# The second group norm's statistics in an attention and conditional-convolution kernel: one ScalarE square around the channel mean instead of VectorE's batch-norm instructions

## Chip, cores and metric

The kernel runs on one NeuronCore of a Trainium2 chip. The metric is the device time of one execution in microseconds; shown are the median and the ends of three runs. The profile is one further execution. In it PE is TensorE, DVE is VectorE, ACT is ScalarE, POOL is GpSimd and SP is SyncE, the engine that issues the transfers.

## What is computed

Sixteen images x of 128 channels and 32x32 pixels pass through two residual blocks. Each block begins with a group norm over 32 groups of four channels. The core of the reference:

```python
x = x + _L0_conv_ref(_gn(x), g1, w_qkv, mem_kv, w_out, b_out, g2)
x = x + _L1_conv_ref(_gn(x), expert_weight, rconv_w, rconv_b, fc_w, fc_b)

def _gn(v, G=32, eps=1e-05):
    g = v.reshape(B_, G, C_ // G, H_, W_)
    m = jnp.mean(g, axis=(2, 3, 4), keepdims=True)
    s = jnp.var(g, axis=(2, 3, 4), keepdims=True)
    return ((g - m) / jnp.sqrt(s + eps)).reshape(v.shape)
```

`_L0_conv_ref` is linear attention with four heads: an RMS norm over channels, projections to q, k and v, a softmax of q over channels and of k over pixels, a context matrix, an output projection and a second RMS norm. `_L1_conv_ref` pools the normed image to 4x4 cells, computes from them three gates per output channel (the routing), mixes three 3x3 filters by these gates, and convolves the image with the mix.

The change concerns the second `_gn`: mean and variance of each channel of the image `x2`, the sum of x and the attention's output. Averages over the four channels of a group are then taken by a small matmul.

## The kernel before

The kernel is a software pipeline over the 16 images, with an order written out by hand for each engine in a function `step(t, p)`. In step t different stages work on different images: the projections and the first norm's application on image t-1, the attention's context and output on image t-2, the second norm, the routing and the filters' mix on image t-3, the convolution on image t-4. An engine takes its instructions strictly in the written order. Between engines there are only semaphores: `do(part, t, p, age)` emits a part for image t-age, and a part begins with its waits. Steps 9 to 14 are a loop of three rounds of two steps; the others are written out. Tiles lie as 128 channels (partitions) by 1024 pixels, or as eight tiles of 128 pixels by 128 channels.

The stretch of a step that the change touches, engine by engine:

- VectorE forms `x2` (`residual1`, L902). Then `gn2_stats` (L904 to L910) takes batch-norm statistics of its two halves, `rms1` (L782) averages eight columns of square sums of another image (GpSimd's `rms1` waits for them, and ScalarE's `qkv_evacuate` for that), and `gn2_aggregate` (L912 to L917) writes mean and variance of each channel to `meanvar[:, 1, :]`. `gn2_pool` (L919) sums `x2` over 4x4 cells for the routing. Then come `means` (L750), which waits for the group means, `k_sums`, `differences`, `gn2_centre`, `spreads` (L766), `context_mask`, `variances` and `mix_evacuate`.
- TensorE's `group_means` (L1099 to L1112) averages the means of four channels each. It waits for `meanvar2_done` and stands between the two halves of `q_transpose` (L1181), behind `key_context_transpose` (L1163). Behind these come `contexts` (L1165 to L1169), which waits for `x_k_done`, then `project` for tile 1, `group_variances`, `mixes`, more projections and `outputs` (L1191). The 54 matmuls of the convolution are strewn between all of these, and the conv matmuls are in the same strict order.
- ScalarE evacuates the key contexts (`k_x_evacuate`, L613), copies the second half of the transposed image (`x_copy`, L575), evacuates the transposed contexts (`x_k_evacuate`, L619, for which `contexts` waits), then the transposed q (L625) and the projected tiles (L594).

Of the kernel before, what the change touches and what calls it, by code (L numbers as in the profile page):

```python
# [25 lines left out]
def attention_condconv_kernel(  # L26
# [38 lines left out]
    with ctx:  # L65
# [6 lines left out]
        def sem(name):  # L72
            return ctx.enter_context(nc.semaphore(name))
# [77 lines left out]
        stats2 = sb("stats2", [128, 2, 6])  # L151
# [69 lines left out]
        stats2_read = sem("stats2_read")  # L221
# [45 lines left out]
        stats2_done = sem("stats2_done")  # L267
# [288 lines left out]
        def _(act):  # L556
# [3 lines left out]
            def squares1(b, p, h):  # L560

                act.wait_ge(x_t_ps, 2 * b + h + 1)
                if past(b, 1):
                    act.wait_ge(ssq1_done, b)
                    act.wait_ge(ssq1_sum_done, 2 * b)
                for t in range(NT // 2 * h, NT // 2 * (h + 1)):
                    last = nc.scalar.activation(squares[:, tile(t)], ps_qkv[h][:, tile(t % (NT // 2))], ACT.Square,  # L567
                                                accum_out=ssq1_sum[:, t:t + 1])
                last.then_inc(ssq1_sum_done, 1)
# [67 lines left out]

            def image_high(b, p):
# [39 lines left out]
            def step(t, p):  # L678
# [18 lines left out]
                do(k_x_evacuate, t, p, 2)  # L697
                do(x_copy, t, p, 1, 1)
# [16 lines left out]
        def _(dve):  # L715
# [188 lines left out]
            def gn2_stats(b, p):  # L904
                dve.wait_ge(x2_done, b + 1)
                if past(b, 1):
                    dve.wait_ge(meanvar2_done, b)
                for h in range(2):
                    last = v.bn_stats(stats2[:, h, :], x2[p][:, half(h)])
                last.then_inc(stats2_done, 1)  # L910

            def gn2_aggregate(b, p):  # L912
                if past(b, 1):
                    dve.wait_ge(gmean_ps, b + GAP)
                    dve.wait_ge(spread_done, b + GAP)
                dve.wait_ge(stats2_done, b + 1).then_inc(stats2_read, 1)
                v.bn_aggr(meanvar[:, 1, :], stats2[:, :, :].rearrange("p h s -> p (h s)")).then_inc(meanvar2_done, 1)  # L917

            def gn2_pool(b, p):  # L919
                dve.wait_ge(x2_done, b + 1)  # L920
                if past(b, 1):
                    dve.wait_ge(pooled_c_done, b)
                v.tensor_reduce(pooled[:, :].rearrange("p (i j) -> p i j", j=SP),
                                x2[p][:, :].rearrange("p (i a j b) -> p i j a b", i=SP, j=SP, b=W // SP), AX.XY, ALU.add).then_inc(pooled_done, 1)

# [97 lines left out]
            def step(t, p):  # L1023
# [8 lines left out]
                do(gn2_stats, t, p, 3)  # L1032
                do(rms1, t, p, 1)
                do(gn2_aggregate, t, p, 3)
                do(gn2_pool, t, p, 3)
# [282 lines left out]
```

## Time and profile before

| what | us |
|---|---|
| median of three runs | 458.72 (458.58 to 461.26) |
| the profiled execution's own time | 460.76 |
| its span, first to last instruction | 459.0 |
| TensorE busy | 413.5 |
| VectorE busy | 356.3 |
| ScalarE busy | 294.7 |
| GpSimd busy | 262.2 |

The profiled execution has 1.76 us outside its span. "Busy" counts the time in which at least one instruction of the engine runs. A timeline row gives start, length, engine, line and operation, with the output left of the arrow; square brackets give idle time ahead of it and what ended that. Lines are those of the kernel before.

### The profile page before, as it was taken

Reading aid. Unit: us, or ns where it says so; the run is one execution under the profiler, and the core shown is the slowest. Engines: PE = TensorE matmul, PEld = TensorE weight load, DVE = VectorE, ACT = ScalarE, POOL = GpSimd, SP = SyncE. Lnnn points to the kernel's source line nnn. Section 1 sums busy time; section 2 is a strip of 40 time slices with the busy share of each in tenths; the row PEclk is TensorE's granted clock in tenths of the full one; section 3 lists DMA queues with packets and bytes.
Section 4 is the critical chain, followed back from the end, with each engine's and each line's share of the span. In section 5 each row is a group of like instructions: output and inputs, shape, how many; then the busy total and the mean of one; then the engine's idle time right before and its main releaser. Section 6 shows DMA issues by size and latency. Waiting matters only on the chain.

```text
span 459.0 us, 8623 instructions
## 1 busy us (share of the span) xinstructions
PE 413.5 (90%) x2478; PEld 358.3 (78%) x2478; DVE 356.3 (78%) x773; ACT 294.7 (64%) x903; POOL 262.2 (57%) x249
## 2 busy tenths in 40 slices
PE   2476686789999999999999999999999999999896
PEld 1466585678989898988888798989898989787675
DVE  3265578979798979888897979898989796977710
ACT  2336566676867686868686787868686868644221
POOL 4326354855758493949494757667684847334130
PEclk9997858699999999999999999999999999999899
DMA  6302024222625243343425061626262423342331
GB/s 194 162 0 94 1 93 183 91 94 91 230 93 217 106 174 149 142 181 128 194 91 230 34 244 43 237 83 228 91 229 91 171 106 131 145 157 120 142 133 46
DMA packets 18786, 61.61 MB, mean 134 GB/s; under 512 B 2992, under 2 KB 4032, under 8 KB 18752
## 3 DMA queue, kind: packets, MB, share of 16 engines
q1 hardware_dynamic: 18752, 61.21, 35.5%
q8 instruction: 15, 0.25, 0.2%
q14 instruction: 19, 0.16, 0.1%
HBM read 19.29 MB, written 8.39 MB: 60 GB/s over the span
## 4 chain that ended last, share of the span: by engine, by line
PE 60%; DVE 13%; issue 10%; ACT 8%; DMA 4%; POOL 1%; SPq 1%; DVEq 0%; ACTq 0%; POOLq 0%
PE ps_conv L1227 26%; PE ps_att L1158 6%; PE ps_y L1191 6%; PE ps_y L1197 3%; PE ps_qkv L1137 3%; PE ps_y L1181 3%; DVE w_full L1008 2%; DMA xa<-in_x_dram 2%; PE ps_qkv L1139 2%; PE ps_qkv L1138 2%; ACT expert_raw L655 2%; DMA expert_raw<-_conv_expert_weight_dram 2%; ACT squares L567 2%; PE ps_qkv L1124 2%; DVE route_terms L956 2%
## 5 line engine op out<-in xcount | busy, mean ns | idle before, releaser
L594 ACT ACTIVATE qk<-ps_qkv,scale 128x256 f32<-128x256 f32 x128 | 56.4, 470 | 10.8 <-PE ps_qkv L1139 8.8
L537 POOL TENSOR_TENSOR left_hi<-zeros 128x32 fp32r<-128x32 f32 x16 | 5.7, 358 | 80.0 <-DMA right_lo<-img_lo 80.0
L661 ACT ACTIVATE w_hi<-w_full 128x1152 fp32r<-128x1152 f32 x16 | 18.7, 1167 | 50.7 <-DVE w_full L1014 50.7
L530 POOL TENSOR_TENSOR w_lo<-w_full,w_hi 128x1152 fp32r<-128x1152 f32 x16 | 42.8, 2677 | 12.7 <-ACT w_hi L661 7.7
L485 POOL TENSOR_TENSOR x_lo<-x,x_hi 128x1024 fp32r<-128x1024 f32 x16 | 38.3, 2393 | 16.1 <-ACT x_hi L584 16.1
L1137 PE MATMUL ps_qkv<-wqk_hi,x_hi 128*128 128x256 f32 x128 | 42.3, 331 | 5.7 <-ACT qk L594 3.7
L511 POOL TENSOR_TENSOR scale<-ssq,minus_half 128x8 f32<-128x8 f32 x16 | 26.2, 1638 | 34.4 <-DVE ssq L883 34.4
L635 ACT ACTIVATE y_scaled<-ps_y 128x128 f32<-128x128 f32 x128 | 33.3, 292 | 14.7 <-PE ps_y L1191 14.7
L1227 PE MATMUL ps_conv<-right_lo,w_hi 128*128 128x512 f32 (+1 forms) x96 | 41.7, 435 | 0.0
L1227 PE MATMUL ps_conv<-img_hi,w_hi 128*128 128x512 f32 x96 | 39.3, 410 | 2.1 <-POOL w_lo L530 1.8
L1227 PE MATMUL ps_conv<-right_hi,w_lo 128*128 128x512 f32 (+1 forms) x96 | 38.7, 403 | 0.0
L1227 PE MATMUL ps_conv<-right_hi,w_hi 128*128 128x512 f32 (+1 forms) x96 | 37.8, 394 | 0.0
L1227 PE MATMUL ps_conv<-left_lo,w_hi 128*128 128x512 f32 (+1 forms) x96 | 37.7, 393 | 0.0
L1227 PE MATMUL ps_conv<-img_hi,w_lo 128*128 128x512 f32 x96 | 37.7, 392 | 0.0
L1227 PE MATMUL ps_conv<-img_lo,w_hi 128*128 128x512 f32 x96 | 37.6, 392 | 0.0
L1227 PE MATMUL ps_conv<-left_hi,w_lo 128*128 128x512 f32 (+1 forms) x96 | 37.5, 390 | 0.0
L1139 PE MATMUL ps_qkv<-wqk_hi,x_lo 128*128 128x256 f32 x128 | 37.3, 292 | 0.0
L1227 PE MATMUL ps_conv<-left_hi,w_hi 128*128 128x512 f32 (+1 forms) x96 | 37.3, 388 | 0.0
L1138 PE MATMUL ps_qkv<-wqk_lo,x_hi 128*128 128x256 f32 x128 | 37.2, 290 | 0.0
L670 ACT ACTIVATE expert_raw<-ps_conv,gmean 128x512 f32<-128x512 f32 x32 | 21.7, 678 | 23.9 <-PE ps_conv L1227 23.8
L567 ACT ACTIVATE squares<-ps_qkv 128x128 f32<-128x128 f32 x128 | 32.4, 259 | 6.8 <-PE ps_qkv L1124 6.8
L1158 PE MATMUL ps_att<-x_nt,k_exp 128*128 128x130 f32 x256 | 34.7, 293 | 0.0
(149 smaller groups left out, 1322.8 us busy)
## 6 DMA issues: line engine op xcount, KB each, us to landing
xa<-in_x_dram SPq DMA_DIRECT2D x16, 512.0 KB, 4.3
xb<-in_x_dram SPq DMA_DIRECT2D x16, 512.0 KB, 4.8
out_dram<-expert_raw SPq DMA_DIRECT2D x16, 512.0 KB, 2.9
left_hi<-img_hi SPq DMA_DIRECT2D x16, 511.5 KB, 3.1
right_hi<-img_hi SPq DMA_DIRECT2D x16, 511.5 KB, 4.0
left_lo<-img_lo SPq DMA_DIRECT2D x16, 511.5 KB, 2.9
right_lo<-img_lo SPq DMA_DIRECT2D x16, 511.5 KB, 3.7
expert_raw<-_conv_expert_weight_dram SPq DMA_DIRECT2D x1, 1728.0 KB, 9.3
```

What stands on the lines that cost most here:

```text
L485: nc.gpsimd.tensor_tensor(x1_lo[:, :], x1[:, :], x1_hi[:, :].bitcast(F32), ALU.subtract).then_inc(x1_lo_done, 1)
L511: nc.gpsimd.tensor_tensor(scale2[:, :], ssq2[:, :], minus_half[:, :], ALU.pow).then_inc(scale2_done, 1)
L530: nc.gpsimd.tensor_tensor(w_lo[p][:, :, :].rearrange("p t o -> p (t o)"), w_full[:, :], w_hi[p][:, :, :].bitcast(F32).rearrange("p t o -> ...
L567: last = nc.scalar.activation(squares[:, tile(t)], ps_qkv[h][:, tile(t % (NT // 2))], ACT.Square, accum_out=ssq1_sum[:, t:t + 1])
L594: nc.scalar.activation(qk[:, t, :], ps_qkv[t % 2][:, 0:QK], ACT.Copy, scale=scale1[:, t:t + 1]).then_inc(qkv_done, 1)
L635: last = nc.scalar.activation(y_scaled[:, t, :], ps_y[:, tile(t)], ACT.Square, accum_out=ssq2_sum[:, t:t + 1])
L1137: mm(o, x1_hi[:, tile(t)], wqk_hi[:, :], start=True, stop=False)
L1138: mm(o, x1_hi[:, tile(t)], wqk_lo[:, :], start=False, stop=False)
L1139: mm(o, x1_lo[:, tile(t)], wqk_hi[:, :], start=False, stop=True).then_inc(qkv_ps, 1)
L1158: last = mm(ps_att[:, 0:CEXT], k_exp[:, t, :], x_nt[p][:, t, :], start=False, stop=(t == NT - 1))
L1191: last = mm(ps_y[:, tile(t)], q_t[p][:, tile(t)], mix[p][:, :], start=True, stop=True)
L1227: last = mm(into, weight[:, tap, :], pixels[:, top + down:bottom + down, :], start=(n == 0), stop=(n == 3 * TAPS - 1))
```

## The change

Mean and variance of a channel no longer come from VectorE's batch-norm instructions. `gn2_pool` moves up to stand directly behind `residual1`. A new `gn2_sum` adds the 16 cell sums of a channel to one number, and a new `gn2_average` writes two multiples of it: the channel's mean to `meanvar[:, 1, 0:1]`, and minus the mean over the square root of N = 1024 to `centre_bias`. A new part on ScalarE, `gn2_variance`, reads all of `x2` once, squares it with scale 1/32 and this bias, and lets the accumulator sum the squares: that sum is the channel's variance. The full-size output goes to `squares`, a scratch tile that the first RMS norm also uses. The part stands between `k_x_evacuate` and the second `x_copy`. `meanvar2_done`, for which TensorE's `group_means` waits, is now raised by it. TensorE's, GpSimd's and SyncE's orders stay as they were.

```diff
@@ ScalarE
             def squares1(b, p, h):
                 act.wait_ge(x_t_ps, 2 * b + h + 1)
+                if past(b, 3):
+                    act.wait_ge(meanvar2_done, b - 2)
...
+            def gn2_variance(b, p):
+
+                act.wait_ge(centre_bias_done, b + 1)
+                act.wait_ge(ssq1_sum_done, 2 * (b + 3) if not isinstance(b, int) else 2 * min(b + 3, B))
+                if past(b, 1):
+                    act.wait_ge(spread_done, b + GAP)
+                nc.scalar.activation(squares[:, :], x2[p][:, :], ACT.Square, bias=centre_bias[:, :], scale=1.0 / N ** 0.5,
+                                     accum_out=meanvar[:, 1, 1:2]).then_inc(meanvar2_done, 1)
...
                 do(k_x_evacuate, t, p, 2)
+                do(gn2_variance, t, p, 3)
                 do(x_copy, t, p, 1, 1)
@@ VectorE
-            def gn2_stats(b, p):
-                dve.wait_ge(x2_done, b + 1)
-                if past(b, 1):
-                    dve.wait_ge(meanvar2_done, b)
-                for h in range(2):
-                    last = v.bn_stats(stats2[:, h, :], x2[p][:, half(h)])
-                last.then_inc(stats2_done, 1)
-
-            def gn2_aggregate(b, p):
-                if past(b, 1):
-                    dve.wait_ge(gmean_ps, b + GAP)
-                    dve.wait_ge(spread_done, b + GAP)
-                dve.wait_ge(stats2_done, b + 1).then_inc(stats2_read, 1)
-                v.bn_aggr(meanvar[:, 1, :], stats2[:, :, :].rearrange("p h s -> p (h s)")).then_inc(meanvar2_done, 1)
-
...
+            def gn2_sum(b, p):
+                dve.wait_ge(pooled_done, b + 1)
+                if past(b, 1):
+                    dve.wait_ge(centre_bias_done, b)
+                v.tensor_reduce(pooled_sum[:, :], pooled[:, :], AX.X, ALU.add).then_inc(pooled_sum_done, 1)
+
+            def gn2_average(b, p):
+
+                dve.wait_ge(pooled_sum_done, b + 1)
+                if past(b, 1):
+                    dve.wait_ge(meanvar2_done, b)
+                    dve.wait_ge(gmean_ps, b + GAP)
+                    dve.wait_ge(dev_done, b + GAP)
+                v.tensor_scalar(meanvar[:, 1, 0:1], pooled_sum[:, :], 1.0 / N, None, ALU.mult)
+                v.tensor_scalar(centre_bias[:, :], pooled_sum[:, :], -1.0 / (N * N ** 0.5), None, ALU.mult).then_inc(centre_bias_done, 1)
...
                 do(residual1, t, p, 3)
-                do(gn2_stats, t, p, 3)
+                do(gn2_pool, t, p, 3)
+                do(gn2_sum, t, p, 3)
+                do(gn2_average, t, p, 3)
                 do(rms1, t, p, 1)
-                do(gn2_aggregate, t, p, 3)
-                do(gn2_pool, t, p, 3)
                 turn(means, t, p, 0)
```

VectorE's row in the program before, in the loop, from the forming of `x2` to the group means (`ssq` is `rms1`'s output, `x_1` is one of the two `x2` buffers):

```order
L902 SCALAR_TENSOR_TENSOR x_1<-ps_y,g_c,xb 128x1024
L909 BN_STATS stats<-x_1 128x6 x2
L787 TENSOR_SCALAR ssq<-ssq_sum 128x8
L917 BN_AGGR meanvar<-stats 128x2
L923 TENSOR_REDUCE pooled<-x_1 128x16
L759 TENSOR_SCALAR nmean<-ps_stat 128x2
```

and in the changed program, where line numbers after the first edits are some lines higher:

```order
L915 SCALAR_TENSOR_TENSOR x_1<-ps_y,g_c,xb 128x1024
L921 TENSOR_REDUCE pooled<-x_1 128x16
L928 TENSOR_REDUCE pooled_sum<-pooled 128x1
L937 TENSOR_SCALAR meanvar<-pooled_sum 128x1
L938 TENSOR_SCALAR centre_bias<-pooled_sum 128x1
L800 TENSOR_SCALAR ssq<-ssq_sum 128x8
L772 TENSOR_SCALAR nmean<-ps_stat 128x2
```

The pooling has moved ahead of `rms1`; two reads of the whole tile by BN_STATS and the BN_AGGR are gone, and three small instructions on one or 16 columns stand in their place. ScalarE's row before, from the results' evacuation in the same step:

```order
L670 ACTIVATE expert_raw<-ps_conv,gmean_1 128x512
L613 ACTIVATE k_x<-ps_att 128x130
L575 ACTIVATE x_nt<-ps_qkv 128x4x128
L619 ACTIVATE x_k<-ps_att 128x128
L625 ACTIVATE q_t<-ps_y 128x512
L594 ACTIVATE qk<-ps_qkv,scale 128x256 x2
L625 ACTIVATE q_t<-ps_y 128x512
```

and in the changed program:

```order
L682 ACTIVATE expert_raw<-ps_conv,gmean_1 128x512
L616 ACTIVATE k_x<-ps_att 128x130
L647 ACTIVATE squares,meanvar<-x_1,centre_bias 128x1024
L578 ACTIVATE x_nt<-ps_qkv 128x4x128
L622 ACTIVATE x_k<-ps_att 128x128
L628 ACTIVATE q_t<-ps_y 128x512
L597 ACTIVATE qk<-ps_qkv,scale 128x256 x2
L628 ACTIVATE q_t<-ps_y 128x512
```

The square on 1024 columns now stands ahead of the second copy to `x_nt`, the evacuation of `x_k` and the evacuation of q.

## Rows read from the trace of the kernel before

**Rows 1.** The page: busy us, share of the span and instructions by engine.

```profile
PE 413.5 (90%) x2478; PEld 358.3 (78%) x2478; DVE 356.3 (78%) x773; ACT 294.7 (64%) x903; POOL 262.2 (57%) x249
```

**Rows 2.** Stretches: length; busy and count of PE, PEld, DVE, ACT, POOL; clock; DMA share, GB/s.

```profile
145.63:169.53 23.90, 23.90 (x154) 21.02 (x154) 20.87 (x47) 17.94 (x57) 15.61 (x15) 1.00 0.39 143
...
241.90:266.71 24.81, 24.16 (x154) 21.00 (x154) 21.32 (x47) 17.86 (x57) 15.58 (x15) 1.00 0.38 143
...
290.79:315.26 24.47, 24.19 (x154) 21.00 (x154) 21.87 (x48) 18.23 (x57) 15.83 (x15) 1.00 0.40 149
```

**Rows 3.** Timeline of VectorE, 162 to 167 us: start, length, engine, line, operation.

```profile
162.76 1.22 DVE L902 SCALAR_TENSOR_TENSOR x<-ps_y,g_c,xb 128x1024 f32<-128x1024 f32 x1
164.02 1.29 DVE L909 BATCH_NORM_STATS2 stats<-x 128x6 f32<-128x512 f32 x2
165.22 0.15 DVE L787 TENSOR_SCALAR ssq<-ssq_sum 128x8 f32<-128x8 f32 x1
165.49 0.21 DVE L917 BATCH_NORM_AGGREGATE meanvar<-stats 128x2 f32<-128x12 f32 x1
165.62 1.20 DVE L923 TENSOR_REDUCE pooled<-x 128x16 f32<-128x1024 f32 x1
166.73 0.15 DVE L759 TENSOR_SCALAR nmean<-ps_stat 128x2 f32<-128x2 f32 x1
```

**Rows 4.** Timeline of TensorE, the same step.

```profile
166.33 0.28 PE L1112 MATMUL ps_stat<-meanvar,group_avg 128*128 128x2 f32 x2
166.47 0.63 PE L1181 MATMUL ps_y<-ident,q_exp 128*128 128x128 f32 x4
166.94 0.41 PE L1168 MATMUL ps_att<-memk_exp,memv_t 128*128 128x128 f32 x2
```

**Rows 5.** Timeline of ScalarE, the same step, and two rows from 160 us.

```profile
160.57 0.25 ACT L567 ACTIVATE squares<-ps_qkv 128x128 f32<-128x128 f32 x1
160.73 0.19 ACT L567 ACTIVATION_READ_ACCUMULATOR squares<-ps_qkv 128x1 f32 x1
...
165.20 0.28 ACT L613 ACTIVATE k_x<-ps_att 128x130 f32<-128x130 f32 x1 [0.34 <-PE ps_att L1158]
165.37 0.60 ACT L575 ACTIVATE x_nt<-ps_qkv 128x512 f32<-128x512 f32 x1
166.53 0.28 ACT L619 ACTIVATE x_k<-ps_att 128x128 f32<-128x128 f32 x1 [0.56 <-PE ps_att L1163]
```

**Rows 6.** Groups by line, the nearest relatives: line, operands, count, busy us, mean ns.

```profile
L813 DVE TENSOR_REDUCE k_max<-ps_att 128x1 f32<-128x128 f32 x16 | 4.5, 281 | 0.0
...
L1021 DVE TENSOR_SCALAR gmean<-nmean 128x1 f32<-128x1 f32 x16 | 2.3, 145 | 0.0
...
L731 DVE TENSOR_REDUCE memk_max<-mem_c 128x1 f32<-128x4 f32 x1 | 0.1, 136 | 0.0
```

**Rows 7.** Groups by line on ScalarE, the nearest relative of the square.

```profile
L642 ACT ACTIVATE img_hi<-x,nmean 128x1024 fp32r<-128x1024 f32 x16 | 18.4, 1149 | 3.3 <-DVE nmean L759 3.3
```

**Rows 8.** Timeline of the step around 91 us, ScalarE and TensorE.

```profile
90.87 0.28 ACT L613 ACTIVATE k_x<-ps_att 128x130 f32<-128x130 f32 x1 [1.74 <-PE ps_att L1158]
...
92.61 0.41 PE L1168 MATMUL ps_att<-memk_exp,memv_t 128*128 128x128 f32 x2
```

**Rows 9.** Timeline of the last two steps of the second norm.

```profile
404.57 1.22 DVE L902 SCALAR_TENSOR_TENSOR x<-ps_y,g_c,xb 128x1024 f32<-128x1024 f32 x1
...
408.28 0.39 PE L1168 MATMUL ps_att<-memk_exp,memv_t 128*128 128x128 f32 x2
...
426.40 0.21 DVE L917 BATCH_NORM_AGGREGATE meanvar<-stats 128x2 f32<-128x12 f32 x1 [0.19 <-DVE stats L909]
...
426.67 0.38 PE L1112 MATMUL ps_stat<-meanvar,group_avg 128*128 128x1 f32 x2
...
427.64 0.15 DVE L759 TENSOR_SCALAR nmean<-ps_stat 128x1 f32<-128x1 f32 x1
```

**Rows 10.** Timeline of VectorE, the latest arrival of an input image.

```profile
243.49 1.28 DVE L740 BATCH_NORM_STATS2 stats<-xa 128x6 f32<-128x512 f32 x2 [2.08 <-DMA xa<-in_x_dram]
```

More of the change, by code:

```diff
@@ L150, in attention_condconv_kernel @@
         x2 = [sb(f"x2_{p}", [128, N]) for p in range(2)]
-        stats2 = sb("stats2", [128, 2, 6])
+        pooled_sum = sb("pooled_sum", [128, 1])
+        centre_bias = sb("centre_bias", [128, 1])
         pooled = sb("pooled", [128, SP * SP])
@@ L220, in attention_condconv_kernel @@
         ssq1_sum_done = sem("ssq1_sum_done")
-        stats2_read = sem("stats2_read")
         x1_done = sem("x1_done")
@@ L266, in attention_condconv_kernel @@
         x2_done = sem("x2_done")
-        stats2_done = sem("stats2_done")
+        pooled_sum_done = sem("pooled_sum_done")
+        centre_bias_done = sem("centre_bias_done")
         meanvar2_done = sem("meanvar2_done")
```

## Prediction

> **What bounds the kernel now.** I read the page's busy shares first. TensorE is busy for 413.5 us of a span of 459.0, 90%; VectorE for 356.3 us (78%), ScalarE for 294.7 (64%) [rows 1]. Then I cut the middle of the run into stretches from one start of `outputs` (L1191) to the next, which is one step of the pipeline. The stretch from 145.63 to 169.53 is 23.90 us long and TensorE is busy for all 23.90 of it, at a granted clock of 1.00 (2.4 GHz). In this step TensorE waits for nobody, and any time that it is made to wait is added to the step. The stretches from 241.90 and from 290.79 are longer, 24.81 and 24.47 us, with 0.65 and 0.28 us in which TensorE has no work [rows 2]. That is the only kind of slack the middle has. So the question is not how much work VectorE loses and ScalarE gains, but when TensorE's next instruction may start.
>
> Last I read the timelines of one full step, engine by engine, around the place of the change. `x2` starts at 162.76, takes 1.22 and is ready at 163.98. The batch-norm statistics start at 164.02 and the aggregate ends at 165.49 + 0.21 = 165.70 [rows 3]. `group_means` runs at 166.33 [rows 4]: it has 0.63 us in hand. Behind it the second half of the q transposes starts at 166.47 and `contexts` at 166.94. ScalarE in the same stretch evacuates `k_x` from 165.20 to 165.48, copies to `x_nt` from 165.37 to 165.97, then waits 0.56 us for the transpose and evacuates `x_k` from 166.53 to 166.81 [rows 5]. `contexts` starts 0.13 us after that. So two chains meet TensorE here, and each has little in hand: statistics to `group_means`, and `k_x` to `x_k` to `contexts`.
>
> **The change, part by part.** *Removed on VectorE:* the statistics (1.29 for the pair) and the aggregate (0.21). *Moved:* the pooling, 1.20 us, which stood behind the aggregate, now stands ahead of everything that `group_means` needs. *Added on VectorE:* one sum over 16 columns and two TENSOR_SCALARs on one column. The trace has no 16-column sum; its bounds are 0.14 us (four columns) and 0.28 (128 columns) [rows 6]. I take 0.16, near the first. A one-column TENSOR_SCALAR takes 0.145 [rows 6]; the second can overlap with the first, so the pair takes between 0.2 and 0.3 and I take 0.23. *Added on ScalarE:* a square on 1024 columns with a bias column. Its nearest relative is `image_high`, with the same input, size and kind of bias, 1.149 us [rows 7]. An accumulating square is followed by a read of the accumulator; on 128 columns that starts 0.09 us ahead of the square's end (160.73 against 160.57 + 0.25) and takes 0.19 [rows 5]. So the pair ends 1.25 us after its start, and the next instruction can start after 1.15.
>
> *The new chain in this step.* `x2` ends at 163.98; the pooling runs from 164.02 to 165.22; the sum ends at 165.42 (0.04 us between dependent instructions, as between `x2`'s end and the statistics' start [rows 3]); the two multiples end at 165.69. ScalarE has been free since 165.48 and starts the square at 165.72. The accumulator is out at 166.97. TensorE follows the last aggregate of the run by 0.06 us (426.40 + 0.21 against 426.67 [rows 9]), so `group_means` starts at 167.03 in place of 166.33: 0.70 later.
>
> *What queues behind the square on ScalarE.* The second `x_nt` copy starts at 166.87 in place of 165.37. It takes 0.60, of which 0.1 is overlapped, so `x_k` starts at about 167.35 and ends at 167.63. `contexts` starts at 167.68 by this path, and by the other at 167.03 + 0.61 (its distance from `group_means` before, 166.94 against 166.33 [rows 4]) = 167.64. Both say 0.74 later. What follows on ScalarE (q's evacuation, the projected tiles) moves by no more than that, and TensorE asks for it 0.74 later too. `rms1` on VectorE slips from 165.22 [rows 3] to about 165.75; GpSimd's reciprocal square root and the scaled evacuation behind it slip by 0.5, less than TensorE. The group means are read by VectorE at about 167.35 instead of 166.73 [rows 3], a slip of 0.6. I cost all of these at nothing, because TensorE's own 0.74 hides them; if that cover were gone, each would cost its own slip. The new waits in `squares1` are for something done most of a step earlier.
>
> *The saved VectorE time.* Per step 1.50 us go and 0.39 come, 1.1 saved. It falls into the time in which VectorE waits for the group means, so I count it at nothing.
>
> Here a page speaks against the small instructions. The row for one column is 0.145 us [rows 6]. The Trainium skill, "VectorE: DVE Perf Modes", section on the TRN2 errata, says that an instruction reading SBUF pays a fixed cost, put at 58 cycles of 0.96 GHz beside its columns, and advises tiles of at least 512 elements so that the cost is spread. An estimate by that page gives 0.08 us for the sum and 0.06 for each multiple, and the step's loss would be some 0.2 us smaller; the page's figure is less than half of the row, the measurement decides, and its advice points the same way as the row.
>
> **The sum.** The second norm runs in 16 steps.
> - Eight are like the one above: 8 x 0.74 = 5.9.
> - In five others `k_x` ends later against `x2`, and ScalarE would have started the square later than VectorE lets it, but all else was later too. In the one at 91 us `k_x` ends at 91.15, the square runs to 92.40, the copy starts at 92.30, `x_k` ends at 93.08, and `contexts` starts at 93.14 in place of 92.61 [rows 8]: 0.53. I take this for all five: 2.7.
> - In the first step of the second norm TensorE is later still: 0.1 by the same working, an estimate from the last case.
> - In the last but one there is no `x_nt` copy and no `rms1`, and TensorE stood at `contexts` at 408.28, 3.71 after the start of `x2` at 404.57 [rows 9]. The new chain puts it at 167.68 - 162.76 = 4.92 after: 1.2.
> - In the last there is no `k_x`. `group_means` slips to `x2` plus 4.3, 427.9 in place of 426.67, but VectorE read it only at 427.64 because the pooling was in the way [rows 9]. Now it reads it at about 428.3: 0.7 on a chain that ends the kernel.
>
> Together 10.6 us. Back come at most the idle 0.65 and 0.28 of rows 2: there an image landed late (VectorE waited 2.08 us for it [rows 10]), and its load is issued ahead of the new delay, so a later TensorE finds it there. I take 0.8. The net is +9.8 us: 460.76 for the profiled execution becomes 470.6, and the median of 458.72, 2.04 below the profiled one, becomes 468.5.
>
> *Bounds of the unknown.* With the lower ends (0.14, 0.2, and a square of 1.05) a step loses about 0.15 less, -2.2 us in all. With the upper ones (0.28, 0.3, 1.25) it loses 0.3 more, +4.5. The forecast's own range is therefore 465.5 to 473.
>
> **Rivals.** A measurement of this kernel can tell about 1% from no change, so the bounds are 463 and 454 us.
> - *Hidden.* The modelled ends of the matmuls make TensorE look fuller than it is, and there is half a microsecond of slack somewhere in each step. Then a step loses 0.1 to 0.2 and the kernel 2 to 4 us with the last steps: 461.5. For it: the ends of the matmuls are modelled, so 23.90 of 23.90 may hold small gaps. Against it: the `k_x` to `contexts` chain gives 0.13 us of room only [rows 4, 5]. 10%.
> - *VectorE pays back: faster.* If VectorE paces the step, from the routing's sums through the filters and the softmax to `x2`, each step gets the 1.1 us that it saves, less the 0.74 lost if ScalarE's square still reaches TensorE, and 16 x 0.4 = 6 us less gives 452. It decides from the point at which VectorE has no idle time around `group_means`. Against it: the work saved stands behind that chain, not in it, and VectorE is busy for only 20.87 of 23.90 [rows 2]. 3%.
> - *The delay spreads.* The square also pushes the scale of the projected tiles and the q evacuation past the point where TensorE needs them, or holds back the shifted images. A second loss of 0.4 us per step gives 16 x 0.4 = 6.4 more: 475. Against it: the slips worked out above are all under 0.74. 11%.
> - *The clock falls.* All stretches of rows 2 have 1.00, the one with 0.65 us of idle TensorE too, so a stall of 0.74 should change nothing. If it did and each of 16 steps ran 2 us at 1.2 GHz, 1 us more per step would give 484. The Trainium skill, "TensorE: Matmul & The Clock Gate", Part 1, says that the array's clock is halved after idle time; this trace shows no such fall at stalls of this size. 1%.
>
> That the change does not do what it says is no likely rival: mean and variance come out of the same numbers, with the same instruction count for TensorE.
>
> **How the numbers follow.** The forecast has 75%: 468.5. The range reaches down into the hidden case and up into the spreading one, 463.0 to 475.0. Slower by over 1%: the forecast, the spreading, the clock, 87%, less a few for a forecast that ends under 463: 0.85. Within 1%: the hidden case and those few, 0.12. Faster: 0.03.
>
> **What would show it.** In the changed profile TensorE should wait at `group_means` or `contexts` in about 15 steps, 0.6 to 0.8 us each, for ScalarE's square or for `x_k`; the square should take 1.15 us and start 0.2 us or so behind the end of `k_x`; the step that was 23.90 us should be 24.6. VectorE should wait for the group means by about 1.4 us, where it waited for nothing. If that step is still under 24.1, the hidden case is right. If TensorE's new waits stand at projections or at the convolution, the delay has spread. If VectorE's end of `x2` comes earlier against TensorE, the saved time was worth something.

## The result and the profile after

The changed kernel takes 469.19 us (median of four runs, 468.44 to 469.82), the kernel before, run beside it, 459.99. The ratio is 1.0195, with a 95% interval of 1.0141 to 1.0248: slower by 9.2 us. The forecast was 468.5, 9.8 above the 458.72 from which it started. The profiled execution took 469.82 us with a span of 468.1; the forecast for it was 470.6. Ratios and intervals leave out runs more than 1.5% above the fastest run of the same kernel; of all kernels here only one, the pooling first with the average early, has such runs.

The page's busy row, which answers to [rows 1]:

```profile
PE 417.4 (89%) x2478; PEld 360.1 (77%) x2478; DVE 339.9 (73%) x773; ACT 311.9 (67%) x935; POOL 266.2 (57%) x249
```

VectorE has 16.4 us less to do and ScalarE 17.2 more, and the span is 9.1 longer. TensorE has the same 2478 matmuls; its busy time is 3.9 us more. The mean granted clock is 0.956 in place of 0.963, and the first matmuls behind a wait show as longer ones (the pair of the group means 0.35 us in place of 0.28); how the 3.9 us divide between the two was not worked out.

Stretches between two starts of `outputs` (now L1205), as in [rows 2] (length; busy and count of PE, PEld, DVE, ACT, POOL; clock; DMA):

```profile
144.92:169.56 24.64, 24.18 (x154) 21.06 (x153) 20.56 (x48) 19.11 (x59) 16.84 (x15) 1.00 0.40 153
...
244.31:269.73 25.42, 24.17 (x155) 21.07 (x153) 20.98 (x48) 19.10 (x59) 16.55 (x15) 1.00 0.38 144
...
294.69:320.06 25.37, 24.26 (x155) 21.03 (x154) 20.95 (x48) 19.14 (x59) 15.85 (x15) 1.00 0.38 143
```

The step that was 23.90 us with TensorE full is 24.64 with 24.18 busy. The two long ones are 25.42 and 25.37 in place of 24.81 and 24.47. They have 0.46, 0.60 and 0.83 us more without work on TensorE than the same steps before; the rest of the loss, at most 0.28 us, shows as longer busy time. The granted clock is 1.00 in all of them.

VectorE's timeline of one step, which answers to [rows 3]:

```profile
162.15 1.22 DVE L915 SCALAR_TENSOR_TENSOR x<-ps_y,g_c,xb 128x1024 f32<-128x1024 f32 x1
163.41 1.22 DVE L921 TENSOR_REDUCE pooled<-x 128x16 f32<-128x1024 f32 x1
164.67 0.17 DVE L928 TENSOR_REDUCE pooled_sum<-pooled 128x1 f32<-128x16 f32 x1
164.87 0.15 DVE L937 TENSOR_SCALAR meanvar<-pooled_sum 128x1 f32<-128x1 f32 x1
164.94 0.14 DVE L938 TENSOR_SCALAR centre_bias<-pooled_sum 128x1 f32<-128x1 f32 x1
165.00 0.22 DVE L800 TENSOR_SCALAR ssq<-ssq_sum 128x8 f32<-128x8 f32 x1
166.85 0.16 DVE L772 TENSOR_SCALAR nmean<-ps_stat 128x2 f32<-128x2 f32 x1 [1.63 <-PE ps_stat L1126]
```

The pooling is behind `x2` at once; the sum (L928) starts 2.52 us after the start of `x2`, the second multiple ends at 2.93. `nmean` now waits 1.63 us for the group means, where [rows 3] had no wait. That is where VectorE's saved time went: in this step it stands idle there. ScalarE in the same step, as in [rows 5]:

```profile
164.69 0.28 ACT L616 ACTIVATE k_x<-ps_att 128x130 f32<-128x130 f32 x1 [0.45 <-PE ps_att L1172]
165.12 1.15 ACT L647 ACTIVATE squares<-x,centre_bias 128x1024 f32<-128x1024 f32 x1
166.18 0.19 ACT L647 ACTIVATION_READ_ACCUMULATOR squares<-x,centre_bias 128x1 f32 x1
166.27 0.58 ACT L578 ACTIVATE x_nt<-ps_qkv 128x512 f32<-128x512 f32 x1
166.75 0.27 ACT L622 ACTIVATE x_k<-ps_att 128x128 f32<-128x128 f32 x1
```

The square starts 0.04 us after `centre_bias`, runs 1.15, and the accumulator is out at 166.37, 4.22 after the start of `x2`. The copy to `x_nt` stands behind it, and `x_k` starts 4.60 after the start of `x2`, where it was 3.77. TensorE, as in [rows 4]:

```profile
166.46 0.35 PE L1126 MATMUL ps_stat<-meanvar,group_avg 128*128 128x2 f32 x2 [0.44 <-issue]
166.68 0.64 PE L1195 MATMUL ps_y<-ident,q_exp 128*128 128x128 f32 x4
167.15 0.40 PE L1182 MATMUL ps_att<-memk_exp,memv_t 128*128 128x128 f32 x2
```

Against the start of `x2` the group means are at 4.31 in place of 3.57 and `contexts` (L1182) at 5.00 in place of 4.18. The view of waits on TensorE says how often:

```profile
PE ps_stat L1126 <- issue: 7.1, 13, 0.9
...
PE ps_stat L1126 <- ACT squares L647: 2.5, 3, 1.2
```

Together 9.6 us in all 16 steps, from 0.16 to 1.24 us each. The "issue" of the first row is not idle sequencing: in the step above the row carries "issue" and yet the matmul starts 0.09 us after the accumulator's read. I read it as a wait whose releaser the profile could not name. The prediction had asked for waits of 0.6 to 0.8 us in about 15 steps. VectorE's side of the same thing (it was 9.0 us in 5 waits before):

```profile
DVE nmean L772 <- PE ps_stat L1126: 35.9, 19, 3.4
```

### The profile page after: what moved, and what is told of

Read it like the earlier page. It is cut to its first block, busy times and chain, and to the rows that moved or that the text cites. A ratio compares the mean times of both kernels' runs of the same rounds, so it can differ in the third digit from the quotient of the medians.

```text
span 468.1 us, 8702 instructions
## 1 busy us (share of the span) xinstructions
PE 417.4 (89%) x2478; PEld 360.1 (77%) x2478; DVE 339.9 (73%) x773; ACT 311.9 (67%) x935; POOL 266.2 (57%) x249
## 4 chain that ended last, share of the span: by engine, by line
PE 66%; DVE 13%; issue 11%; ACT 5%; DMA 2%; SPq 1%; POOL 1%; DVEq 0%; ACTq 0%
PE ps_conv L1241 29%; PE ps_y L1205 6%; PE ps_att L1172 6%; PE ps_y L1195 3%; PE ps_y L1211 3%; PE ps_qkv L1151 3%; PE ps_qkv L1153 2%; PE ps_qkv L1152 2%; DVE w_full L1022 2%; ACT expert_raw L667 2%; DMA expert_raw<-_conv_expert_weight_dram 2%; PE ps_stat L1218 2%; ACT qk L597 2%; PE ps_qkv L1138 1%; PE ps_stat L1126 1%
## 5 line engine op out<-in xcount | busy, mean ns | idle before, releaser
L538 POOL TENSOR_TENSOR left_hi<-zeros 128x32 fp32r<-128x32 f32 x16 | 7.1, 447 | 80.5 <-DMA right_lo<-img_lo 80.5
L1241 PE MATMUL ps_conv<-left_hi,w_lo 128*128 128x512 f32 (+1 forms) x96 | 37.9, 394 | 0.0
```

The source lines that it names most:

```text
L1241: last = mm(into, weight[:, tap, :], pixels[:, top + down:bottom + down, :], start=(n == 0), stop=(n == 3 * TAPS - 1))
```

## The experiments

All runs are compared with the kernel before on the same chip. `x2`+4.3 means 4.3 us after the start of `x2` in that step. "Over the twelve steps" means from the start of the third `x2` to that of the last but one, in the profiled execution: 290.28 us before and 298.96 in the changed kernel, 8.7 more. Behind some medians this length is given, because the stretch ahead of the third `x2` varies from kernel to kernel by more than the steps do (see the end).

**Pooling first.** Is the lateness of the statistics alone enough?

```diff
                 do(residual1, t, p, 3)
+                do(gn2_pool, t, p, 3)
                 do(gn2_stats, t, p, 3)
-                do(rms1, t, p, 1)
                 do(gn2_aggregate, t, p, 3)
-                do(gn2_pool, t, p, 3)
+                do(rms1, t, p, 1)
```

> The kernel before with one edit in VectorE's order: the pooling stands ahead of the batch-norm statistics, and the averaging of the square sums behind the aggregate, as in the change. ScalarE has no new work. Theory (the loss is lateness of the channel statistics and of x_k at TensorE): the aggregate ends 1.1 us later, about 4.1 us after the start of x2, so the group means start 4.15 after it in place of 3.57, TensorE waits 0.6 us there in most of the 16 steps, and the time is 8 us above the kernel before. Rival (the loss is ScalarE's square in its queue alone, the group means had room): no change within 2 us, and no wait at the group means.

Measured: 469.5 us, ratio 1.0215 (1.0148 to 1.0282). So a mere change of order on VectorE, with no new work anywhere, costs as much as the whole change (10.6 us over the twelve steps). Its waits on TensorE:

```profile
PE ps_stat L1112 <- issue: 4.0, 10, 0.6
...
PE ps_stat L1112 <- DVE meanvar L917: 2.4, 3, 1.1
```

That is 6.4 us at the group means, in 13 steps; they start at `x2`+4.16, as worked out. The rival is out. But `outputs` was 0.7 to 0.85 us late, not 0.6, and the time 2 us over what was expected.

**The same with the average of the square sums early.** One line differs: `do(rms1, t, p, 1)` stands between `gn2_stats` and `gn2_aggregate` again.

> The pooling-first run cost 10 us, not 8: TensorE started the group means 0.6 us late but the outputs 0.8 to 0.85 late. Its averaging of the square sums stood behind the aggregate, 1.7 us later than before. Here it stands ahead of the aggregate, as in the kernel before, and the pooling still stands first. Theory (the extra 0.15 to 0.2 us per step came from that averaging, through GpSimd's reciprocal root to ScalarE's scaled evacuations): group means at about 4.2 us after the start of x2, outputs 0.65 later than before and not 0.85, the time 1.5 to 3 us under the pooling-first run. Rival (the extra comes from the late group means themselves, by way of the spreads): the outputs stay 0.85 late and the time is the same within 1 us.

Measured: median of all ten runs 466.29 us, ratio 1.0109 (1.0061 to 1.0156). The group means are still at `x2`+4.16, `outputs` at 7.24 in place of 7.45 to 7.60. So the extra did come with the late average; that it goes by way of GpSimd and the scaled evacuations was expected and not looked at by itself. The ten runs fall into two groups, five from 461.6 to 464.3 and five from 468.2 to 469.4, and the profile, 468.92, is of the upper one. So the size of the gain is not told by the median. The steps tell it: over the twelve steps this kernel loses 5.7 us, 4.9 less than the run before.

**A square beside.** Is what queues behind the square on ScalarE enough? The statistics stay on VectorE; the sum of this square is read by nobody.

```diff
+            def square_beside(b, p):
+
+                act.wait_ge(x2_done, b + 1)
+                act.wait_ge(ssq1_sum_done, 2 * (b + 3) if not isinstance(b, int) else 2 * min(b + 3, B))
+                if past(b, 1):
+                    act.wait_ge(beside_done, b)
+                nc.scalar.activation(squares[:, :], x2[p][:, :], ACT.Square, bias=g2_c[:, :], scale=1.0 / N ** 0.5,
+                                     accum_out=unused_sum[:, :]).then_inc(beside_done, 1)
...
                 do(k_x_evacuate, t, p, 2)
+                do(square_beside, t, p, 3)
```

> The kernel before with the statistics as they were, and beside them a full-size ScalarE square with accumulator at the changed kernel's place, behind the evacuation of k_x, whose sum nobody reads. Only what queues behind it on ScalarE is late. Theory: the square starts when the k_x evacuation ends, 2.7 us after the start of x2, the evacuation of x_k starts 4.35 after it in place of 3.77, and the contexts 4.7 in place of 4.18: 0.5 us in each of 15 steps, so 7 us above the kernel before, with TensorE's wait at the contexts and none at the group means. Rival (only the wait for the statistics costs): no change within 2 us. If this and the pooling-first run each give 7 to 8, the two paths run side by side in the change and do not add up, since the change costs 9 to 10.

Measured: 464.58 us, ratio 1.0122 (1.006 to 1.0185), 5 us and not 7. In the usual step the square starts at `x2`+2.61, `x_k` at 4.22 and `contexts` at 4.55, 0.36 late. I had started the square at the end of the `k_x` evacuation; ScalarE overlaps two instructions by 0.1 us, at both ends of the square. TensorE's wait stands where it should, at `contexts`, short but in 14 steps:

```profile
PE ps_att L1182 <- ACT x_k L623: 2.8, 14, 0.3
```

**Half the square.** Does the loss follow the square's length? (The variance is that of half the image's sum; the rest is as in the change.)

```diff
-                nc.scalar.activation(squares[:, :], x2[p][:, :], ACT.Square, ...
+                nc.scalar.activation(squares[:, 0:N // 2], x2[p][:, 0:N // 2], ACT.Square, ...
```

> The changed kernel with the square over only the first 512 of 1024 pixels of each channel; the variance is then that of half the image's sum. Theory (a step's loss follows the square's length): the square is 0.43 to 0.5 us shorter, group means and contexts come earlier by as much, each of 16 steps loses 0.3 in place of 0.75, and the time is 7 us under the changed kernel, about 462 where before is 460. Rival (what costs is the longer VectorE chain and the extra semaphore hand-over, not the square's length): under 2 us less than the changed kernel.

Measured: 460.99 us, ratio to before 1.0037 (1.0002 to 1.0072), 8 us under the changed kernel, where 7 were expected. The square takes 0.72 in place of 1.15 us, and group means and `contexts` come at `x2`+3.88 and 4.57, each 0.42 us earlier. Over the twelve steps the kernel loses 3.6 us in place of 8.7: 0.43 us less per step, which is the time by which the square is shorter. The other 3 us or so lie outside these steps: in its profile the third `x2` starts at 108.28, in that of the changed kernel at 112.71.

**Wait for the mean only.** The group means read `meanvar[:, c, 0]`, the mean; the variance is first read by `spreads`.

```diff
-                    pe.wait_ge(meanvar2_done, j + 1 - GAP)
+                    pe.wait_ge(centre_bias_done, j + 1 - GAP)
...
             def spreads(j, p):
...
+                if past(j, GAP):
+                    dve.wait_ge(meanvar2_done, j + 1 - GAP)
```

> The changed kernel with the wait put where the number is needed: TensorE's group means read only the mean, so they wait for VectorE's average, and VectorE's spreads, which read the variance, wait for the square. The square stays at its place on ScalarE. Theory (two paths side by side): the group means start at 3.57 after the start of x2 as before and TensorE does not wait there, but the evacuation of x_k still starts at 4.6, so the contexts start at 4.9 to 5.0 as in the changed kernel: the wait moves from the group means to the contexts and the time stays within 2 us of the changed kernel's 469. Rival (the wait at the group means is the whole cost): 7 to 9 us less, the time of before.

Measured: 467.45 us, ratio 1.019 (1.0128 to 1.0253). The group means are at `x2`+3.57 again, TensorE waits there for nobody, and `contexts` is at 4.91. The wait has moved one place on, nearly whole:

```profile
PE ps_att L1184 <- ACT x_k L622: 8.3, 15, 0.9
```

With the pooling-first run this is the core of the matter. Over the twelve steps the late `x_k` alone costs 7.9 us (here; 3.1 with the square beside, which starts earlier), the late statistics alone 5.7 (with the average early), and both together 8.7: they run side by side and do not add up. In time, 467.45 is 1.7 us under the changed kernel, which the intervals of the two do not tell from nothing.

**The square one place further back.** Built on the mean-wait kernel: `do(gn2_variance, t, p, 3)` stands behind `do(x_k_evacuate, t, p, 2)`.

> The mean-wait kernel with the square moved one place further back on ScalarE, behind the copy to x_nt and the evacuation of x_k. Theory: x_k is evacuated at 3.77 as before and the contexts start at 4.18, but the square now runs from 3.95 to 5.1 after the start of x2, so q's evacuation and the first scaled evacuation are 1.1 us late and the third projection waits for about 0.45 us, and the spreads for the variance: TensorE's wait moves on, 0.5 us per step, and the time is 3 to 4 us under the mean-wait kernel, 464. Rival (only what stands ahead of the contexts matters): the time of before, 460.

Measured: 499.74 us, ratio 1.0897 (1.0821 to 1.0974). I was wrong by 36 us. `contexts` was on time at `x2`+4.18; all of the loss was behind it. The wait that had grown (4.3 us in 5 waits before):

```profile
PE ps_stat L1133 <- DVE spread L787: 31.1, 18, 2.2
```

Two us per step, for an instruction on one column. Over the twelve steps these waits are 24.2 us of the 37.9 that the kernel loses. Most of the rest is the clock: behind eight of the twelve waits it fell to half, with TensorE full, for at least 3.2 us each. One of them, less than a us behind a wait that ended at 120.02:

```profile
120.87:124.07 3.20, 3.20 (x17) 3.13 (x16) 1.50 (x4) 0.95 (x2) 1.89 (x3) 0.50 0.76 306
```

At half the clock 3.2 us of matmuls take 1.6 us longer than at the full one, so eight such stretches come to some 13 us (an estimate from these rows). VectorE's row in one step, for the pair of spreads, and then GpSimd's:

```profile
173.59 2.07 DVE L787 SCALAR_TENSOR_TENSOR spread<-dev,meanvar 128x1 f32<-128x1 f32 x2 [0.58 <-ACT squares L647]
```

```profile
173.74 1.89 POOL L498 TENSOR_TENSOR x_nt<-x_nt,scale 128x1024 f32<-128x1024 f32 x1
```

The spreads begin 0.15 us ahead of GpSimd's scaling of `x_nt` and end at 175.66; that scaling ends at 175.63. The second spread, 0.2 us long elsewhere, ends only with it. The late square had pushed the spreads, which waited for the variance, into this operation; whether that holds them up is what the next run asks.

**GpSimd's scaling held.** The late-square kernel, with one wait more:

```diff
             def x_scale(b, p):
                 pool.wait_ge(x_nt_done, 2 * (b + 1))
                 pool.wait_ge(scale1_done, b + 1)
+                pool.wait_ge(spread_done, b + 2)
```

> The kernel of the late-square run cost 40 us where 4 were expected: TensorE waited 2.0 us per step at the group variances for VectorE's spreads, of which the second, on one column, took up to 1.93 us and ended within 0.05 us of the end of GpSimd's scaling of x_nt in nearly every step. Here GpSimd's scaling waits until the spreads are done; nothing else changes. Theory (a VectorE instruction on two or more SBUF operands stands still while GpSimd's operation runs, once that has begun): the spreads take 0.35 us for the pair, the group variances start at 5.7 after the start of x2, TensorE waits 0.4 to 0.5 us per step, and the time is 466 to 469. Rival (the spreads are late because the variance is, whatever GpSimd does): 490 or more, and the spreads stay long.

Measured: 462.99 us, ratio 1.0081 (1.0049 to 1.0113): one wait added on another engine gives back 37 us, the clock's share with it: over the twelve steps it is 1.00 again. The groups of the spreads by line, first without that wait, then with it (count, busy us, mean ns):

```profile
L787 DVE SCALAR_TENSOR_TENSOR spread<-dev,meanvar 128x1 f32<-128x1 f32 x32 | 29.0, 937 | 13.7 <-ACT squares L647 13.6
```

```profile
L788 DVE SCALAR_TENSOR_TENSOR spread<-dev,meanvar 128x1 f32<-128x1 f32 x32 | 6.4, 231 | 13.8 <-ACT squares L648 13.5 <-issue 0.2
```

and TensorE's wait at the group variances, 31.1 us before:

```profile
PE ps_stat L1134 <- DVE spread L788: 7.8, 17, 1.0
```

The time is 3 us under what I had expected, but the steps are not: over the twelve they lose 6.0 us, 0.5 each, as expected. What is shorter lies ahead of them: the third `x2` starts at 109.45, before at 114.29.

**The copy on VectorE.** Built on the mean-wait kernel; the second `x_nt` copy leaves ScalarE for VectorE, behind `rms1`.

```diff
-                do(x_copy, t, p, 1, 1)
...
+            def x_copy_high(b, p):
+                if past(b, 2):
+                    dve.wait_ge(k_x_ps, b - 1)
+                dve.wait_ge(ssq1_sum_done, 2 * b + 2)
+                dve.wait_ge(x_nt_done, 2 * b + 1)
+                v.tensor_copy(x_nt[p][:, NT // 2:NT, 0:C], ps_qkv[1][:, :].rearrange("p (t c) -> p t c", c=C)).then_inc(x_nt_done, 1)
```

> The mean-wait kernel with the second x_nt copy moved from ScalarE to VectorE, where about 1 us was saved, behind the averaging of the square sums. Theory (the x_k evacuation starts when the square and the copy behind the k_x evacuation are through): the evacuation of x_k starts at 4.1 after the start of x2 in place of 4.6, contexts at 4.45, the step loses 0.3 us against before, and the time is 6 to 7 us under the mean-wait kernel, 461. Rival (VectorE has no room for 0.6 us there): contexts as in the mean-wait kernel or later, time not below 466.

Measured: 461.31 us, ratio 1.0039 (0.9995 to 1.0083). `x_k` starts at `x2`+4.12 and `contexts` at 4.42, and the step is 24.25 us (2.7 us lost over the twelve steps). As expected.

**The copy and `x_k` on VectorE.** In addition the evacuation of `x_k` becomes a `v.tensor_copy` on VectorE, behind `x_copy_high`, with the same waits.

> The kernel of the copy run with the evacuation of x_k on VectorE too, so that nothing for which TensorE waits before the contexts stands behind the square. Theory (the loss is only lateness of the mean and of x_k, and TensorE is full otherwise): contexts at 4.2 to 4.3 after the start of x2, no wait of TensorE there, a step of 24.1 us as before, and the time of before within 2 us, 459 to 461; no gain over it, though VectorE has less to do, since TensorE is full. Rival 1 (the larger ScalarE load costs by itself): 463 or more. Rival 2 (the saved VectorE time is worth something once the waits are gone): under 456.

Measured: 454.94 us, ratio 0.9922 (0.9879 to 0.9965). `contexts` is at `x2`+4.19, there is no wait of TensorE left at it or at the group means, and the stretch that answers to the full step of [rows 2] is

```profile
162.98:186.90 23.92, 23.92 (x155) 21.02 (x153) 20.78 (x49) 18.63 (x57) 15.86 (x15) 1.00 0.39 147
```

23.92 us long, all of it busy. Over the twelve steps it takes 290.20 us, before 290.28. So the whole loss of the change is gone with the two late inputs, though ScalarE still does the square. The time is 4 us below the kernel before. The theory had 459 to 461 and failed in that; it is rival 2's number, under 456. But rival 2's reason, VectorE's time, would show in the middle steps, and these are as long as before; what stays open stands at the end.

**The moves alone.** The kernel before with both moves to VectorE, between the aggregate and the pooling, and the batch-norm statistics as they were.

> The kernel before, statistics as they were on VectorE, with the second x_nt copy and the evacuation of x_k moved from ScalarE to VectorE between the aggregate and the pooling, as in the kernel that came out 4 us under before. Theory (VectorE has the room for these two only where the statistics have left it): the copy and the evacuation take 0.9 us, the pooling ends at 5.1 after the start of x2 in place of 4.1, the group means are read at 5.1 and the spreads end at 5.6 to 5.7, so the group variances wait 0.4 us per step, and the time is 464 to 467. Rival (the gain of that kernel came from the moves alone): 453 to 456.

Measured: 471.88 us, ratio 1.0257 (1.018 to 1.0334), 13 us slower. The waits at the group variances are twice what I had put there:

```profile
PE ps_stat L1130 <- DVE spread L770: 14.7, 18, 1.0
```

So the moves are no gain by themselves, at least at this place ahead of the pooling: the room for them on VectorE is what the change had freed.

**Both, and the scaling held.**

> The kernel that came out 4 us under before, with GpSimd's scaling of x_nt held until VectorE's spreads are done. Theory (in that kernel TensorE is full in the middle steps, and a step is 24.0 us): within 1.5 us of that kernel's 455, since the spreads were not waited for there. Rival (the spreads' long forms still cost there): 2 us or more less.

Measured: 454.33 us, ratio 0.9885 (0.9809 to 0.996), 0.6 us from the run without the extra wait. Where the spreads are early enough, holding GpSimd gives nothing. (It takes 289.87 us over the twelve steps.) These two kernels are the ones that beat both before and after.

## Why the prediction was right

**What bounds the kernel.** Right. TensorE was full in the middle steps, and whatever held it back was added. The strongest evidence is the pooling-first run: no work added, 10 us lost.

**The chain of one step.** Nearly row by row. The steps of the prediction, with what was measured in the step from 162.15: pooling 1.20 (1.22), sum 0.16 (0.17), the pair of multiples 0.23 (0.21), square started 2.96 after `x2`'s start (2.97), read out at 4.21 (4.22), group means at 4.27 (4.31), `x_k` at 4.59 (4.60), `contexts` at 4.92 (5.00). The groups by line over all 16:

```profile
L647 ACT ACTIVATE squares<-x,centre_bias 128x1024 f32<-128x1024 f32 x16 | 18.4, 1149 | 5.8 <-DVE centre_bias L938 5.6
...
L647 ACT ACTIVATION_READ_ACCUMULATOR squares<-x,centre_bias 128x1 f32 x16 | 3.0, 187 | 0.0
```

```profile
L928 DVE TENSOR_REDUCE pooled_sum<-pooled 128x1 f32<-128x16 f32 x16 | 2.7, 170 | 0.5
...
L937 DVE TENSOR_SCALAR meanvar<-pooled_sum 128x1 f32<-128x1 f32 x16 | 2.5, 154 | 0.5
...
L938 DVE TENSOR_SCALAR centre_bias<-pooled_sum 128x1 f32<-128x1 f32 x16 | 2.3, 144 | 0.0
```

The nearest relatives were the right ones: `image_high` had 1149 ns, and so has the square. The 58 cycles of the Trainium skill, "VectorE: DVE Perf Modes", section on the TRN2 errata, would have made these small instructions 0.06 to 0.08 us, less than half of what they take here. The same section says that the 58 is too low for a large copy, where a fixed term of about 150 cycles was measured; an estimate with that term gives 0.16 us for one column and 0.17 for 16, and these rows are close to it.

**The two paths side by side.** The prediction had both at 0.7 and took the later one, not the sum. The pooling-first, square-beside and mean-wait runs confirm it one by one.

**The sum over the steps.** Here three terms were mis-sized. They do not cancel: the middle and the end grew by 10.5 us, where 9.8 was forecast, and a head that was 1.4 us shorter in this profile brought the whole to 9.1. That part of the agreement is luck. The run in three parts, cut at the start of the first and of the last but one `x2`, before and after (columns as in [rows 2]):

```profile
0.00:61.45 61.45, 34.97 (x181) 30.42 (x181) 30.77 (x64) 29.03 (x96) 26.49 (x40) 0.88 0.27 89
61.45:404.57 343.12, 331.56 (x2072) 290.01 (x2073) 301.09 (x652) 250.13 (x775) 222.89 (x194) 0.98 0.38 144
404.57:459.00 54.43, 46.95 (x226) 37.90 (x225) 24.42 (x59) 15.56 (x35) 12.78 (x16) 0.97 0.32 126
```

```profile
0.00:60.02 60.02, 34.43 (x181) 29.70 (x181) 31.15 (x65) 28.96 (x96) 26.53 (x40) 0.87 0.27 92
60.02:411.67 351.65, 334.68 (x2072) 291.33 (x2073) 286.07 (x653) 265.04 (x803) 226.86 (x194) 0.97 0.37 140
411.67:468.10 56.43, 48.30 (x226) 39.10 (x225) 22.70 (x59) 17.94 (x39) 12.81 (x16) 0.94 0.31 122
```

The middle part grew by 8.53 us, where 8.7 less the regained 0.8, so 7.9, was forecast, and the end by 2.0, where 1.9 was forecast. The head, in which the change has nothing, was 1.4 us shorter.
- *The six steps of the loop lose more than 0.74.* There the square starts 0.14 to 0.2 us later than in the steps that are written out, in one of them:

```profile
287.05 1.22 DVE L915 SCALAR_TENSOR_TENSOR x<-ps_y,g_c,xb 128x1024 f32<-128x1024 f32 x1
...
289.84 0.14 DVE L938 TENSOR_SCALAR centre_bias<-pooled_sum 128x1 f32<-128x1 f32 x1
...
290.16 1.15 ACT L647 ACTIVATE squares<-x,centre_bias 128x1024 f32<-128x1024 f32 x1 [0.39 <-DVE centre_bias L938]
...
292.18 0.41 PE L1182 MATMUL ps_att<-memk_exp,memv_t 128*128 128x128 f32 x2
```

`centre_bias` ends at 2.93 after the start of `x2`, the square starts at 3.11, not at 2.97, and `contexts` at 5.13. The prediction had 0.04 us for the hand-over. It is 1.0 us over six steps. That the square waits on three counts, which in the loop are compared with register values, may be why; this was not tried by itself.
- *The early step lost nothing.* For the one at 91 us, 0.53 was charged by [rows 8]. After, `k_x` itself came at 90.68, 4.45 behind the start of `x2` in place of 3.25, and the step from `outputs` to `outputs` there is 26.65 us in place of 26.86. TensorE waits in the early steps for other things, and the square stands in their shade. Of the four others charged alike, one lost 0.30 by its stretch and the three that lie in the loop 0.68 to 0.89. In these three `k_x` had ended at `x2`+2.77 to 2.88, ahead of the 2.96 at which VectorE lets the square start, so the prediction's reason for charging less did not hold for them.
- *Less came back.* The late image of [rows 10] does arrive in time now (VectorE's wait of 2.08 us is gone), but TensorE's step there still went from 24.81 to 25.42, and the other from 24.47 to 25.37. The other looped steps lost 0.68 to 0.89 each, so at most 0.3 us came back, not 0.8.

**The last two steps.** Forecast 1.2 and 0.7:

```profile
416.64 0.39 PE L1182 MATMUL ps_att<-memk_exp,memv_t 128*128 128x128 f32 x2
...
436.09 0.38 PE L1126 MATMUL ps_stat<-meanvar,group_avg 128*128 128x1 f32 x2 [1.24 <-ACT squares L647]
...
436.51 0.16 DVE L772 TENSOR_SCALAR nmean<-ps_stat 128x1 f32<-128x1 f32 x1 [1.75 <-PE ps_stat L1126]
```

`contexts` is 4.97 after the start of `x2` (411.67), where it was 3.71: 1.26. In the last, the group means are read 4.74 after the start of `x2` (431.77), where it was 4.03: 0.71. The end part is not these waits alone: TensorE's time without work grew there by only 0.65 us and its busy time by 1.35. After the last `x2` the clock was at 1.2 GHz for about 6.8 us (437.4 to 444.2), before for about 3.4 (429.4 to 432.8); out of the middle of either, after and then before:

```profile
437.60:444.30 6.70, 6.33 (x16) 4.75 (x17) 4.00 (x15) 1.71 (x3) 0.71 (x2) 0.51 0.40 159
```

```profile
429.80:432.50 2.70, 2.70 (x7) 2.19 (x8) 1.53 (x7) 0.00 (x0) 0.00 (x0) 0.50 0.88 361
```

The prediction had left the clock out of its end, and how much of the 2.0 us it is stays open.

**The rivals.** Hidden slack: out, there was none. VectorE pays back: out in the change's steps; the pooling-first run, with all of VectorE's work, loses the same. Whether it pays in the first two steps stays open (see the end). The delay spreads: not in the change, but it is what cost the extra in the pooling-first run (late average) and most of the 41 us in the late-square run. The clock: 1.00 over the twelve steps of the changed kernel, with stalls at the group means of up to 0.86 us; it did fall at the end, and behind the stalls of 2 us of the late-square run.

## What to carry to other kernels

When the busiest engine is full and in order, price a change by when its inputs are ready, not by the work moved: ask for each instruction that it waits for what now stands ahead of it, on both engines, and take the later path, not the sum. A wait belongs at the first reader of the number: here the mean was needed well ahead of the variance. And in the steps, where TensorE is full, work freed on another engine gained nothing until it was spent: the kernel with the square came out under the kernel before only after the two small evacuations that queued behind it had been given to the engine with the new room.

## What the runs showed of the hardware

A VectorE instruction on one column took up to 1.93 us. In the kernel before the spreads' pair takes 0.81 us where GpSimd's product for the routing starts 0.16 to 0.18 us behind the pair's start, and 0.34 where it starts 0.24 us behind or later. Once, at 93.11, the pair took 2.33 us and ended 0.02 us behind GpSimd's scaling of `x_nt`. In the late-square run the pairs of the first 14 steps all ended within 0.2 us, five of them within 0.05, of the end of that scaling (the last two have none to meet), and a wait that kept the two apart cut the mean of a spread from 937 to 231 ns and the time by 37 us. The Trainium skill, "SBUF — State Buffer", section "Who interferes with whom", says that a VectorE instruction with two SBUF inputs contends with a GpSimd instruction that reads SBUF, and that whichever is issued first keeps the shared port while the other waits until it is through. By that page the second spread, with its inputs in SBUF, waits for the whole of GpSimd's operation; the traces agree. Neither the prediction nor the expectation of the late square took it into account; in the change itself TensorE's waits stand at the group means and not at the spreads.

TensorE's clock fell from 2.4 to 1.2 GHz behind eight of the twelve waits of about 2 us in the late-square run, and behind none of the waits at the group means of 0.22 to 0.86 us in the changed kernel's twelve steps.

What stays open: where the best kernel's 4 us come from. They are not in the steps, which take what they took before. They lie ahead of the third `x2`, which starts at 107.53 and 109.17 us in the profiles of the two kernels with both moves, and at 114.29 before. But that start varies from kernel to kernel: from 111.8 to 115.3 in the five with the old statistics, from 107.5 to 112.7 in the eight with the new. So the new statistics may gain 3 us or so in the head and the first two steps, which would be VectorE's saved time after all. One profile of each does not show it, since the first `x2` alone starts anywhere from 57.85 to 60.99 us in four kernels whose code up to there is the same. One piece is visible: of the 6.8 us between 107.53 and 114.29, 2.0 are in the step from the second to the third `x2`, where before the spreads were held by GpSimd for 2.33 us and in the best kernel take 0.34. The medians of 10 and 25 runs, and the second such kernel's four, say that the gain is real; its cause was not settled.
